# State-space input of a hybrid block: order of moments, normalisation, products and selection rows

## The reference, cut to what matters

```python
xn = _layernorm(x)                                  # 4096 tokens x 256
x_bc = einsum('bld,dn->bln', xn, W_bc)              # 32 columns: B and C
dt_low = einsum('bld,dr->blr', xn, W_dt)            # 64 columns
delta = softplus(einsum('blr,rd->bld', dt_low, W_dtproj) + b_dtproj)
A_bar = exp(delta[..., None] * -exp(A_log))         # the scan, after this part
Bx = (delta * xn)[..., None] * B_sel[:, :, None, :]
```

## Time and profile before

| what | us |
|---|---|
| three timed runs: median (lowest to highest) | 2824.32 (2820.84 to 2824.39) |
| the profiled execution's own time | 2818.2 |
| its span | 2816.4 |
| mean granted TensorE clock, share of full speed | 0.924 |

### The profile page before, as it was taken

How to read it: one execution, slowest core, us unless ns; L and a number is a source line. 1 busy time by engine, 2 the same in 40 slices (tenths; PEclk the granted TensorE clock), 3 DMA queues, 4 the chain that set the end, 5 groups by cost and what they waited for, 6 DMA issues and landing times. The chain is left out here.

```text
span 2816.4 us, 45524 instructions
## 1 busy us (share of the span) xinstructions
PE 2393.2 (85%) x14814; PEld 1062.7 (38%) x14814; DVE 2239.1 (80%) x3665; ACT 1706.4 (61%) x3494; POOL 981.9 (35%) x745
## 2 busy tenths in 40 slices
PE   8898999999999999999995799936476676679991
PEld 5322222222222222222224578822122222357881
DVE  7898999999999999999934854426699999785443
ACT  4247888888888888888881433326556566443330
POOL 4500000000000000000020277756599999427772
PEclk9879999999999999999997799966699999879996
DMA  5405111111111111111145459963234344246997
GB/s 161 137 26 175 43 34 50 50 35 41 51 50 34 43 50 49 30 47 51 28 131 187 143 157 269 240 97 57 57 110 113 106 112 111 85 142 160 270 237 204
DMA packets 255164, 293.70 MB, mean 104 GB/s; under 512 B 39120, under 2 KB 210448, under 8 KB 254928
## 3 DMA queue, kind: packets, MB, share of 16 engines
q1 hardware_dynamic: 213664, 235.09, 28.3%
q0 software_dynamic: 33104, 46.42, 8.8%
q10 hardware_dynamic: 8160, 9.32, 1.0%
HBM read 223.35 MB, written 66.75 MB: 103 GB/s over the span
## 5 line engine op out<-in xcount | busy, mean ns | idle before, releaser
L746 DVE TENSOR_REDUCE att_mx<-att_pR 128x1 f32<-128x512 f32 x2048 | 1266.6, 684 | 34.0 <-PE att_pR L786 33.8
L729 ACT ACTIVATE att_probs<-att_pS 128x512 f32<-128x512 f32 x2048 | 1063.9, 603 | 231.4 <-PE att_pS L816 231.2
L833 PE MATMUL att_pA<-att_probs,att_vh 128*17 128x512 f32 x4096 | 539.7, 599 | 12.6 <-ACT att_acc_sb L710 12.2
L816 PE MATMUL att_pS<-att_q,att_k 64*128 64x512 bf16 x1344 | 458.9, 380 | 0.2 <-ACT att_probs L729 0.2
L2339 PE MATMUL sc_pY<-sc_hc,all_ident 128*128 128x512 f32 x512 | 260.2, 633 | 127.9 <-DVE sc_hc L2296 103.7
L673 POOL TENSOR_TENSOR att_neg<-att_mx,att_minus 128x16 f32<-128x16 f32 x32 | 7.1, 221 | 842.4 <-DVE att_mx L754 842.4
L2205 POOL TENSOR_TENSOR sc_bh<-ssm_du,sc_b 128x1024 f32<-128x1024 f32 x128 | 297.5, 2354 | 9.0 <-DVE sc_hc L2296 4.8
L786 PE MATMUL att_pR<-head_k,head_q 64*128 64x512 bf16 x704 | 258.3, 404 | 14.5 <-PEq L72 7.7
L816 PE MATMUL att_pS<-head_q,head_k 64*128 64x512 bf16 (+1 forms) x1408 | 263.2, 380 | 0.2
L816 PE MATMUL att_pS<-att_qs,att_ks 64*128 64x512 bf16 x1344 | 260.9, 378 | 0.2
L786 PE MATMUL att_pR<-att_ks,att_qs 64*128 64x512 bf16 x672 | 259.2, 386 | 0.1
(11 more groups left out here) (321 smaller groups left out, 3621.1 us busy)
## 6 DMA issues: line engine op xcount, KB each, us to landing
sc_b<-scan_rows SPq DMA_DIRECT2D x128, 256.0 KB
f_wgu<-in_w_gate SPq DMA_DIRECT2D x128, 192.0 KB
f_wgu<-in_w_up SPq DMA_DIRECT2D x128, 192.0 KB
expert_sum<-att_zeros SPq DMA_DIRECT2D x4, 4224.0 KB, 21.2
f_wd<-in_w_down SPq DMA_DIRECT2D x128, 128.0 KB
sc_c<-scan_rows SPq DMA_DIRECT2D x40, 256.0 KB
head_q<-query_parts SPq DMA_DIRECT2D x132, 64.0 KB, 2.3
head_k<-key_parts SPq DMA_DIRECT2D x132, 64.0 KB, 2.2
```

What stands on the lines that cost most here:

```text
L729: act.activation(probs[:, k % (2 * HALF), :], bank(place(k)), ACT.Exp, scale=float(DK) ** -0.5).then_inc(expd, 1)
L746: dve.tensor_reduce(mx4[s][:, k // QC, k % QC:k % QC + 1], pR[:, (s + k) % 3, :], AX.X, ALU.max).then_inc(maxed, 1)
L816: mm = pe.matmul(bank(place(k)), kk[rows, t * P:(t + 1) * P], q[rows, c * GROUP:(c + 1) * GROUP], start=not half, stop=bool(half))
L833: mm = pe.matmul(pA[32 * c:32 * c + DK + 1, :], vh[s][:, t, :], probs[:, (HALF * g + j) % (2 * HALF), :], start=(t == 0), stop=(t == KT - ...
```

## The change

`mom`, `rstd` and `shift` get four buffers. On GpSimd the merging is issued one group further ahead, a turn becomes rounding(n), merges(n+5), product(n), scales(n+4), and the memset of `sel` and the three select_rows stand at the end of turns 0 to 3. On VectorE moments go two groups further ahead and stand between softplus and positive. On ScalarE norm runs two groups ahead, and copy_xnT(n+1) comes straight after low(n). On TensorE turn_group(n+1) comes ahead of the product for B and C. No instruction is added or removed.

```diff
--- before.py
+++ after.py
@@ -1770,6 +1770,7 @@
 
 
 def phase_ssm_in(nc, io, tag, x_sb, sums, ident, xnT, delta, du, bc3, negA, dcol, sel, bc_dram):
+    MOMENTS = 4
     with ExitStack() as ctx:
         m = Mem(nc, ctx, tag)
         wdt = m.sb("wdt", [P, DC, DT_RANK])
@@ -1778,10 +1779,10 @@
         bcol = m.sb("bcol", [P, DC])
         alog = m.sb("alog", [P, DC, STATES])
         stats = m.sb("stats", [P, GT, 6])
-        mom = m.sb("mom", [P, 2, 6, GT])
+        mom = m.sb("mom", [P, MOMENTS, 6, GT])
         mhalf = m.sb("mhalf", [P, GT])
-        rstd = m.sb("rstd", [P, 2, GT])
-        shift = m.sb("shift", [P, 2, GT])
+        rstd = m.sb("rstd", [P, MOMENTS, GT])
+        shift = m.sb("shift", [P, MOMENTS, GT])
         xn = m.sb("xn", [P, GT, D])
         low = m.sb("low", [DT_RANK, GROUP])
         bc_row = m.sb("bc_row", [BC, 2, GROUP])
@@ -1868,7 +1869,7 @@
                 pool.dma_start(x_sb[:, n * GT:(n + 1) * GT, :], src[:, n * GT:(n + 1) * GT, :], accum_op=ALU.add)\
                     .then_inc(merged[q][n], 16)
 
-            MERGED = 3
+            MERGED = MOMENTS + 1
 
             def merges(n):
                 if n + 1 < GROUPS:
@@ -1882,10 +1883,10 @@
                     .then_inc(consts, 1)
 
             def scales(n):
-                s = n % 2
+                s = n % MOMENTS
                 pool.wait_ge(var_ready, n + 1)
-                if n >= 2:
-                    pool.wait_ge(xn_ready, GT * (n - 1))
+                if n >= MOMENTS:
+                    pool.wait_ge(xn_ready, GT * (n - MOMENTS + 1))
                 pool.tensor_tensor(rstd[:, s, :], mom[:, s, 5, :], mhalf[:, :], ALU.pow).then_inc(rstd_ready, 1)
                 pool.wait_ge(rstd_ready, n + 1)
                 pool.tensor_tensor(shift[:, s, :], mom[:, s, 4, :], rstd[:, s, :], ALU.mult).then_inc(shift_ready, 1)
@@ -1908,22 +1909,22 @@
             scales(0)
             merges(2)
             scales(1)
-            pool.memset(sel[:, :, :], 0.0).then_inc(consts, 1)
+            merges(3)
+            scales(2)
+            merges(4)
             for n in range(GROUPS):
-
-                if n:
-                    product(n - 1)
+                rounding(n)
+                if n == 0:
+                    scales(3)
                 if n + MERGED < GROUPS:
                     merges(n + MERGED)
-                if n + 2 < GROUPS:
-                    scales(n + 2)
-                if n:
-                    rounding(n)
-                if n < 3:
-                    select_rows(n)
+                product(n)
+                if n + MOMENTS < GROUPS:
+                    scales(n + MOMENTS)
                 if n == 0:
-                    rounding(0)
-            product(GROUPS - 1)
+                    pool.memset(sel[:, :, :], 0.0).then_inc(consts, 1)
+                elif n < 4:
+                    select_rows(n - 1)
             pool.wait_ge(du_ready, GROUPS)
             pool.wait_ge(consts, 5)
 
@@ -1948,6 +1949,7 @@
 
             norm(0)
             copy_xnT(0)
+            norm(1)
             for n in range(GROUPS):
                 s = n % 2
                 act.wait_ge(projected, n * 2 + 1)
@@ -1955,7 +1957,9 @@
                     act.wait_ge(dt_done, n)
                 act.activation(low[:, :], pL[0:DT_RANK, :], ACT.Copy).then_inc(low_ready, 1)
                 if n + 1 < GROUPS:
-                    norm(n + 1)
+                    copy_xnT(n + 1)
+                if n + 2 < GROUPS:
+                    norm(n + 2)
                 act.wait_ge(projected, n * 2 + 2)
                 if n >= 2:
                     act.wait_ge(bc_ready, n * 2 - 2)
@@ -1966,8 +1970,6 @@
                 act.activation(bc_row[:, s, :], pB[0:BC, s, :], ACT.Copy).then_inc(row_ready, 1)
                 act.wait_ge(hi_ready, n + 1)
                 act.activation(cols(bc3, n)[0:BC, :], bc_hi[0:BC, s, :], ACT.Copy).then_inc(hi_placed, 1)
-                if n + 1 < GROUPS:
-                    copy_xnT(n + 1)
                 act.wait_ge(dt_done, n + 1)
                 if n:
                     act.wait_ge(e_ready, n)
@@ -1997,9 +1999,9 @@
             def moments(n):
                 own = Chain(dve, dve_own, n * OWN_LN)
                 dve.wait_ge(merged[1][n], 16)
-                if n >= 2:
-                    dve.wait_ge(shift_ready, n - 1)
-                layer_norm_stats(dve, own, [x_sb[:, n * GT + j, :] for j in range(GT)], stats, mom[:, n % 2, :, :],
+                if n >= MOMENTS:
+                    dve.wait_ge(shift_ready, n - MOMENTS + 1)
+                layer_norm_stats(dve, own, [x_sb[:, n * GT + j, :] for j in range(GT)], stats, mom[:, n % MOMENTS, :, :],
                                  var_ready, half=-0.5)
                 assert own.n == OWN_LN
 
@@ -2041,14 +2043,16 @@
 
             moments(0)
             moments(1)
+            moments(2)
             parts(0)
             positive(0)
+            moments(3)
             for n in range(GROUPS):
-                if n + 2 < GROUPS:
-                    moments(n + 2)
                 if n + 1 < GROUPS:
                     parts(n + 1)
                 softplus(n)
+                if n + MOMENTS < GROUPS:
+                    moments(n + MOMENTS)
                 if n + 1 < GROUPS:
                     positive(n + 1)
             dve.wait_ge(delta_ready, GROUPS)
@@ -2077,14 +2081,14 @@
                     mm = pe.matmul(pL[0:DT_RANK, :], wdt[:, c, :], cols(xnT, n)[:, c, :],
                                    start=(c == 0), stop=(c == DC - 1))
                 mm.then_inc(projected, 1)
+                if n + 1 < GROUPS:
+                    turn_group(n + 1)
                 if n >= 2:
                     pe.wait_ge(bc_ready, n * 2 - 2)
                 for c in range(DC):
                     mm = pe.matmul(pB[0:3 * BC, n % 2, :], wbc[:, c, :], cols(xnT, n)[:, c, :],
                                    start=(c == 0), stop=(c == DC - 1))
                 mm.then_inc(projected, 1)
-                if n + 1 < GROUPS:
-                    turn_group(n + 1)
                 pe.wait_ge(low_ready, n + 1)
                 if n:
                     pe.wait_ge(pos_ready, n * 2)
```

## The result

Five timed runs of the changed kernel have a median of 2810.05 us (2808.53 to 2813.62), five of the kernel before 2822.49 (2819.21 to 2824.39): ratio 0.9963, 95% interval 0.9952 to 0.9975. It is faster by 12.4 us. (The three runs of the kernel before that were known ahead are among its five.) The profiled executions took 2810.05 and 2818.2, spans 2808.3 and 2816.4.

A forecast was written before the change was run, and what follows sets the result against it. No engine was full; a 16.64 us ring of waits across engines set the stage. 1919.0 + 44.5 + 27.8 + 7.3 = 1998.6 against 2012.14, 13.5 less, gave 2810.8 us, range 2800 to 2817.

The forecast's parts named there:

- The old ring: Chain of waits across engines through moments, pow, shift, norm, turning, product for delta and size: 16.64 us a turn.
- Start: Stage start up to size(0): moments(2) and norm(2) now come first, so size(0) at 1895.3, a loss of 1.3 us.
- Turn 0: From size(0) to lost(1), with the memset holding e1(1): 23.7 us, so lost(1) starts at 1919.0.
- Turns 1 to 3: Turns with a select, which holds e1 because it comes too late: 14.8 us each, 44.5 in all.
- Turns 4 to 6: Turns with nothing left to merge, scale or select: 9.3 us each, 27.8 in all.
- End: From lost(7) to the end of product(7), same order as before: 7.3 us.
- Sum: Stage's last product ends at 1998.6 instead of 2012.14, 13.5 us less; time 2810.8 us.
- Rival 1: e1 slips in ahead of the select: 2.0 us less in each of four turns, 2802.8 us; chance 0.16.
- rival 2: PE at 1.2 GHz or a late landing of group 2 takes part of the gain: 2815 us; chance 0.10.
- rival 3: DVE waits for DMA landings in turns 0 to 3, making it slower: 2834.8 us at 22 us landings; chance 0.04.
- rival 4: A missed wait, such as norm(n+2) behind turning of n+1, keeps the 16.64 us turns: 2824, no change; chance 0.04.
- The rule beside the rows: On VectorE, small moments operations with two SBUF inputs also held by GpSimd: some 0.4 us in four turns, 2812.4 us.

The follow-up runs named there:

- norm late: ScalarE's norm(n+2) moved from ahead of bc_hi(n) to behind bc3(n), against the changed kernel: stage 132.29 us, median 2806.40 us.
- parts from PSUM: Cast and copy of parts made as differences that read PSUM, against the changed kernel: stage 134.76 us, median 2807.08 us.
- Small table: Memset and selects on a 96 x 32 table, spread by ScalarE at the end, against the changed kernel: stage 127.85 us, median 2799.91 us.

## Why the prediction was right

**The old ring** set the 16.6 us turns, and the new order of VectorE and GpSimd, which takes moments, pow and shift out of it, is the whole gain. The prediction named norm and turning as the other half of what is taken out. The run with only VectorE's and GpSimd's order changed shows that they weren't needed for it: 135.3 against 136.6. What GpSimd's own reordering (rounding ahead of product) does without the earlier moments wasn't run.

**Start**: size(0) was forecast 1.3 later, measured 32.6 against 30.9 after the first issue, 1.7 later. **Turn 0**: lost(1) was forecast at 1919.0, 55.9 after the first issue; it came at 57.4, 1.5 late. 0.4 of that is size(0)'s. e1(0) ended 3.9 after size(0), not 3.3, since the parts(0) ahead of it had to wait for bc_hi(0), now right before size(0). And the moments beside lost(0) and beside product(0) took from bn_stats to pow 3.3 each, not 2.8.

**Turns 1 to 3**: forecast 3 x 14.8 = 44.5, measured 15.19 + 14.64 + 14.62 = 44.5. The sum is right and its terms are not; that it fits to a tenth is luck. The step that failed is e1 coming too late for the select and being held by it: it was not. In turn 2: moments 3.3 instead of 2.8 (+0.5), the select 4.29 instead of 3.83 (+0.5), lost 2.50 instead of 2.34 (+0.2), e1 after the select 0 instead of 0.6 with its hand-over (-0.6), and from the end of lost to the next moments 3.3 (1941.78 to 1945.08) instead of 3.9 (-0.6), because the cast had been held by the select already, and behind lost only the end of the copy, the last part, fixed and delta were left.

**Turns 4 to 6**: forecast 27.8, measured 27.4. **End**: 7.3 and 7.3. **Sum**: 13.5 less was forecast, 12.5 measured in the stage, 12.4 between the medians. The forecast of 2810.8 lies closer to the 2810.05 measured than its gain does, and that too is luck: the median of the kernel before is 1.8 lower with five runs than with three, and the gain 1.1 smaller.

**Rival 1** is the one whose premise came true, with its sign (selects with an e1 of 0.7 beside them), and whose price did not. e1 did slip in ahead of the select in turns 1 to 3 (0.69, start 0.07 to 0.10 ahead), only the memset caught it (4.13). The 2.0 a turn were not gained, since parts, which was to run beside the select, waited for bc_hi behind norm; and the runs with norm late show that even without this wait the cast and the copy are held instead. The rest did not happen. TensorE's clock (rival 2) did not stretch turns 4 to 6, and there was no late landing: group 2 landed at 1892.05 less 1866.65 = 25.4 after the first issue, where 24.9 was forecast. After the first three groups bn_stats waited for no DMA (rival 3), and norm waited for no shift in turns 4 to 6 (rival 4).

**The rule beside the rows**, that operations with two inputs in SBUF are held too: the traces agree. The first sum of the moments took 1.11 beside a product and 0.17 alone, some 0.9 a turn and not 0.4, and in the kernel with parts from PSUM the last part took 2.02 instead of 0.68 beside lost. By that rule the forecast was 2812.4, by the rows alone 2810.8. That 2810.05 was measured doesn't speak against the rule: its cost is in the turns, and other terms and the lower median of the kernel before outweigh it.

## What to carry to other kernels

Take a step out of the longest ring, then ask which ring is next and what stands in it only by its place in a queue: here a memset and three selects that nothing in this stage reads cost 0.8 us in the old order as measured (some 1.9 less the landing) and 8.7 in the new one. On one engine, a step that has to wait for another engine belongs behind the short steps that others wait for: norm ahead of bc_hi cost 8.5 us with the selects gone and 4.3 with them. Small table and norm late together give 2792.8 us, 30 under the kernel before, where the change alone gives 12.4.

## What the runs showed of the hardware

The holding goes both ways. An e1 that began 0.10 ahead of a select kept its own time (0.69), and the select grew from 3.83 to 4.29. A cast that ended 0.30 us into lost made lost grow from 2.34 to 2.50. The other way round, the held operation ends nearly the same time after GpSimd's wherever it is held: some 0.55 for e1, 0.28 for the cast, 0.15 for the copy behind lost.

Who wins can't be read off two starts that are within 0.1 us. In the changed kernel the e1 that starts 0.07 ahead of the memset was held through all of it (4.13), and so it was in each of the five profiles with the full memset and an e1 0.06 to 0.07 ahead of it. An e1 0.07 ahead of the third select kept its own time (0.68). In the kernel with parts from PSUM an e1 that starts 0.02 behind a select was not held (0.69), while one 0.04 behind the third select was:

```profile
1960.44 3.83 POOL L1881 TENSOR_SCALAR_AFFINE_SELECT ssm_sel<-ssm_sel 96x4096 bf16<-96x4096 bf16 x1
```

```profile
1960.48 4.34 DVE L2032 TENSOR_SCALAR si_e<-si_e 128x1024 f32<-128x1024 f32 x1
```

So an order that rests on such a gap is not a safe one.

An operation with two inputs in SBUF is held too, a small one (1.11 against 0.17) and a larger one (2.02 against 0.68), while bn_stats (1.40) and operations on PSUM were not. And two short operations in a row can be held by two different GpSimd operations, one each: 3.35 and 2.31 us for work of 0.42 and 0.28.

The stage's first DMA was issued at 1862.5 to 1870.4 us in these profiles, with the same program ahead of it. That is as much as many of the differences here. The stage's own length is the better measure, to within the 1.3 us by which the landings at its start differ.
